# Five of eight batches' queries turned through DRAM instead of one, returning in two lots, with GpSimd taking two of the four low parts

## What is computed

```python
x = x + xattn(v=ctx, k=ctx, q=layernorm(x), mask, W_merge, b_merge)
#   scores = q @ k^T / sqrt(512); masked scores = -1e9; att = softmax(scores)
#   atted = att @ v; result = einsum('bdl,ol->bdo', atted^T, W_merge) + b_merge
x = x + ffn(layernorm(x), clip_x, clip_down, w_gate, w_up, w_down)
#   xq = fake_quant(x); h = fake_quant(silu(xq @ Wg^T) * (xq @ Wu^T)); h @ Wd^T
#   weights are fake-quantised row by row, activations by one scale over all 8 batches
```

## Time and profile before

| | us |
|---|---|
| median of 3 runs | 531.74 |
| lowest, highest | 531.61, 533.95 |
| the profiled execution's own time | 531.5 |
| its span, first to last instruction | 529.7 |
| PE busy | 522.4 (99%) |
| DVE busy | 440.1 (83%) |
| ACT busy | 302.2 (57%) |
| POOL busy | 151.0 (29%) |
| TensorE clock granted, mean | 1.000 of 2.4 GHz |

### The profile page before, as it was taken

The page is one execution under the profiler, slowest core; times in us unless marked ns, Lnnn a source line. Parts: engine busy times, 40 slices in busy tenths (PEclk is TensorE's granted clock), DMA queues, the critical chain, the costliest instruction groups (busy, mean ns, idle before and its releaser), DMA issues. The chain is left out here.

```text
span 529.7 us, 7450 instructions
## 1 busy us (share of the span) xinstructions
PE 522.4 (99%) x2481; PEld 347.0 (66%) x2481; DVE 440.1 (83%) x825; ACT 302.2 (57%) x455; POOL 151.0 (29%) x101
## 2 busy tenths in 40 slices
PE   7999999999999999999999999999999999999997
PEld 6888788888888888888888444444444445444444
DVE  5798999969799698898678678778788787699985
ACT  4795766657647565576433754653654533977620
POOL 2369556555457453663231000000000000000000
PEclk9999999999999999999999999999999999999999
DMA  8929569885884957756467639677301101869785
GB/s 271 262 101 162 189 170 165 255 177 175 197 149 175 223 173 179 178 199 188 103 89 189 239 94 283 244 203 228 112 8 40 40 0 30 341 251 395 270 285 197
DMA packets 80768, 95.71 MB, mean 181 GB/s; under 512 B 36448, under 2 KB 57312, under 8 KB 78176
## 3 DMA queue, kind: packets, MB, share of 16 engines
q1 hardware_dynamic: 80592, 95.24, 64.6%
q10 hardware_dynamic: 144, 0.07, 0.0%
HBM read 60.82 MB, written 26.48 MB: 165 GB/s over the span
## 5 line engine op out<-in xcount | busy, mean ns | idle before, releaser
L1528 PE MATMUL gu<-hid,gu_T 128*128 128x512 f16 x496 | 111.3, 379 | 0.1
L1528 PEld LDWEIGHTS gu<-hid,gu_T 128*128 128x128 f16 x496 | 48.4, 98 | 58.9 <-DVE hid L1394 0.6
L1295 ACT ACTIVATE hid<-gu,gu_mul 128x512 f32<-128x512 f32 x63 | 43.2, 685 | 53.8 <-PE gu L1528 46.8
L1394 DVE SCALAR_TENSOR_TENSOR hid<-gu,gu_mul,hid 128x512 f32 (+1 forms) x63 | 47.0, 748 | 28.4 <-PE gu L1528 16.2
L1410 DVE TENSOR_REDUCE hmax<-hid 128x1 f32 (+2 forms) x48 | 52.7, 1110 | 1.3 <-DVE hid L1394 1.3
L1333 ACT ACTIVATE h<-hid,inv 128x512 int8<-128x512 f32 (+3 forms) x35 | 44.3, 1343 | 11.7 <-DVE gu_T L1447 11.7
L493 ACT ACTIVATE probs<-probs,nmax 128x512 f32<-128x512 f32 x32 | 23.0, 720 | 45.7 <-DVE nmax L692 45.7
L968 PE MATMUL mm<-cT_hi,qT_hi 128*128 128x512 f32 x124 | 48.8, 393 | 0.0
L970 PE MATMUL mm<-cT_hi,qT_lo 128*128 128x512 f32 x124 | 48.3, 390 | 0.0
L969 PE MATMUL mm<-cT_lo,qT_hi 128*128 128x512 f32 x124 | 48.3, 389 | 0.0
L968 PE MATMUL mm<-g_hi,c_hi 128*128 128x512 f32 x124 | 48.2, 389 | 0.0
(11 more groups left out here) (196 smaller groups left out, 1047.0 us busy)
## 6 DMA issues: line engine op xcount, KB each, us to landing
h_dram<-hid SPq DMA_DIRECT2D x3, 2816.0 KB, 9.3
hid<-h_dram SPq DMA_DIRECT2D x3, 2816.0 KB, 11.5
cb<-in_ctx_dram SPq DMA_DIRECT2D x28, 256.0 KB, 8.0
cx<-in_ctx_dram SPq DMA_DIRECT2D x7, 1024.0 KB, 10.7
x<-in_x_dram SPq DMA_DIRECT2D x5, 1024.0 KB, 6.1
x_dram<-x SPq DMA_DIRECT2D x20, 256.0 KB, 2.8
xq<-x_dram SPq DMA_DIRECT2D x5, 1024.0 KB, 10.4
x<-x_dram SPq DMA_DIRECT2D x5, 1024.0 KB, 5.0
```

What stands on the lines that cost most here:

```text
L1295: nc.scalar.activation(silu[SILU_AT[i]], gu[2 * (i % 3)][:], ACT.Silu, scale=gu_mul[:, 0, i:i + 1]).then_inc(silu_done, 1)
L1394: nc.vector.scalar_tensor_tensor(hid[:, b % SLOTS, i * L:(i + 1) * L], gu[2 * (i % 3) + 1][:], gu_mul[:, 1, i:i + 1], silu[SILU_AT[i]], AL ...
L1528: last = nc.tensor.matmul(gu[2 * (i % 3) + g][:], gu_T[:, g, h, i * P:(i + 1) * P], xT[p][:, h, :], start=h == 0, stop=h == T - 1)
```

## The change

Batches 3 to 7 now take the way over DRAM (batch 2 and those before it don't). The queries of a batch come back in two lots of two tiles, four DMAs of 128 KB each, in place of four times four DMAs of 64 KB. SP's order becomes: all four tiles out, x1 tiles 0 and 1 stored, lot 0 back, x1 tiles 2 and 3 stored, lot 1 back, and then x of n+2 as before. Low parts 0 and 1 stay on DVE; 2 and 3 go to POOL, behind `make_c_lo(n)` and ahead of `make_rstd2(n-1)`. `norm1` of the next batch waits for both pairs of low parts.

```diff
-    BLOCK_Q = range(B - 1, B)
+    BLOCK_Q = range(B - 5, B)
...
+                def block_halves(n):
+                    return T // 2 * (n - BLOCK_Q[0])
...
-                    def queries_back(n, t):
-                        pieces = q_dram[n - BLOCK_Q[0], t * P:(t + 1) * P, :].rearrange("(k j) (a f) -> a j k f", j=BLK, f=P)
-                        sp.wait_ge(q_out[t], 16 * (n - BLOCK_Q[0] + 1))
+                    def queries_back(n, h):
+                        rows = slice(h * T // 2 * P, (h + 1) * T // 2 * P)
+                        pieces = q_dram[n - BLOCK_Q[0], rows, :].rearrange("(t k j) (a f) -> a j t k f", j=BLK, k=P // BLK, f=P)
+                        for t in HALF_ROWS[h]:
+                            sp.wait_ge(q_out[t], 16 * (n - BLOCK_Q[0] + 1))
                         for a in range(P // BLK):
-                            sp.dma_start(qn[a * BLK:(a + 1) * BLK, t, :].rearrange("j (k f) -> j k f", f=P),
-                                         pieces[a]).then_inc(q_back[t], 16)
+                            sp.dma_start(qn[a * BLK:(a + 1) * BLK, h * T // 2:(h + 1) * T // 2, :].rearrange(
+                                "j t (k f) -> j t k f", f=P), pieces[a]).then_inc(q_back[h], 16)
...
                     def queries_by_blocks(n):
-                        for t in range(T - 1):
+                        for t in range(T):
                             queries_out(n, t)
+                        for t in HALF_ROWS[0]:
+                            store_x1(n - 2, t)
                         queries_back(n, 0)
-                        queries_out(n, T - 1)
-                        for t in range(1, T):
-                            queries_back(n, t)
+                        for t in HALF_ROWS[1]:
+                            store_x1(n - 2, t)
+                        queries_back(n, 1)
...
                             if n + 1 in BLOCK_Q:
                                 queries_by_blocks(n + 1)
-                            for t in range(T):
-                                store_x1(n - 1, t)
+                            else:
+                                for t in range(T):
+                                    store_x1(n - 1, t)
...
+                    def block_query_lo(n, t):
+                        gp.wait_ge(q_hid, block_queries(n) + t + 1)
+                        nc.gpsimd.tensor_tensor(columns(qT_lo, t), blocks(qn[:, t, :]), columns(qT_hi, t).bitcast(F32),
+                                                ALU.subtract).then_inc(q_split_far, 1)
...
                         make_c_lo(n)
+                        if n + 1 in BLOCK_Q:
+                            for t in HALF_ROWS[1]:
+                                block_query_lo(n + 1, t)
                         if n:
                             make_rstd2(n - 1)
...
                     def block_query_turn(n, t):
-                        dve.wait_ge(q_back[t], 64 * (n - BLOCK_Q[0] + 1))
+                        if t % (T // 2) == 0:
+                            dve.wait_ge(q_back[2 * t // T], 64 * (n - BLOCK_Q[0] + 1))
                         nc.vector.transpose(qn[:, t, :], qn[:, t, :]).then_inc(q_turned, 1)
...
-                                if n + 1 in BLOCK_Q and k >= T // 2:
-                                    for t in HALF_ROWS[k - T // 2]:
+                                if n + 1 in BLOCK_Q and k == T // 2:
+                                    for t in HALF_ROWS[0]:
                                         block_query_lo(n + 1, t)
                                 mixed_lo(n, k)
...
                         if n in BLOCK_Q:
-                            pe.wait_ge(q_split, block_queries(n) + k + 1)
+                            if k < T // 2:
+                                pe.wait_ge(q_split, block_halves(n) + k + 1)
+                            else:
+                                pe.wait_ge(q_split_far, block_halves(n) + k - T // 2 + 1)
```

More of the change, by code:

```diff
@@ L155, in attention @@
                 t_done, t_hi, t_lo = sem("t_done"), sem("t_hi"), sem("t_lo")
-                q_out, q_back = [sem(f"q_out{t}") for t in range(T)], [sem(f"q_back{t}") for t in range(T)]
-                q_turned, q_hid, q_split = sem("q_turned"), sem("q_hid"), sem("q_split")
+                q_out, q_back = [sem(f"q_out{t}") for t in range(T)], [sem(f"q_back{h}") for h in range(2)]
+                q_turned, q_hid = sem("q_turned"), sem("q_hid")
+                q_split, q_split_far = sem("q_split"), sem("q_split_far")
                 wm_done, wm_hid, wm_ready = sem("wm_done"), sem("wm_hid"), sem("wm_ready")
@@ L279, in queries_out, with next_x @@
                         sp.dma_start(q_dram[n - BLOCK_Q[0], t * P:(t + 1) * P, :], qn[:, t, :]).then_inc(q_out[t], 16)
-                    def queries_back(n, t):
-                        pieces = q_dram[n - BLOCK_Q[0], t * P:(t + 1) * P, :].rearrange("(k j) (a f) -> a j k f", j=BLK, f=P)
-                        sp.wait_ge(q_out[t], 16 * (n - BLOCK_Q[0] + 1))
-                        for a in range(P // BLK):
-                            sp.dma_start(qn[a * BLK:(a + 1) * BLK, t, :].rearrange("j (k f) -> j k f", f=P),
-                                         pieces[a]).then_inc(q_back[t], 16)
+                    def queries_back(n, h):
[3 more added lines that the diff above has]
+                            sp.wait_ge(q_out[t], 16 * (n - BLOCK_Q[0] + 1))
+                        for a in range(P // BLK):
+                            sp.dma_start(qn[a * BLK:(a + 1) * BLK, h * T // 2:(h + 1) * T // 2, :].rearrange(
+                                "j t (k f) -> j t k f", f=P), pieces[a]).then_inc(q_back[h], 16)
+                    def next_x(n):
+                        if n:
+                            sp.wait_ge(min2, T * n)
+                            sp.wait_ge(x_free[(n - 1) % 3], 64 * ((n - 1) // 3 + 1))
+                        else:
+                            sp.wait_ge(wm_done, T)
+                        load_x(n + 2)
                     def queries_by_blocks(n):
-                        for t in range(T - 1):
+                        for t in range(T):
                             queries_out(n, t)
+                        for t in HALF_ROWS[0]:
+                            store_x1(n - 2, t)
                         queries_back(n, 0)
-                        queries_out(n, T - 1)
-                        for t in range(1, T):
-                            queries_back(n, t)
+                        for t in HALF_ROWS[1]:
+                            store_x1(n - 2, t)
+                        queries_back(n, 1)
                     def load_x(n):
@@ L361, in _ @@
                                 queries_by_blocks(n + 1)
-                            for t in range(T):
-                                store_x1(n - 1, t)
+                            else:
+                                for t in range(T):
+                                    store_x1(n - 1, t)
                         if n < B - 2:
[L365 to L370, removed]
+                            next_x(n)
                             sp.wait_ge(cT_ready, T * (n + 1))
@@ L517, in norm1 @@
                             if n - 1 in BLOCK_Q:
-                                act.wait_ge(q_split, block_queries(n))
+                                act.wait_ge(q_split, block_halves(n))
+                                act.wait_ge(q_split_far, block_halves(n))
                             else:
```

## The result

| | before | after |
|---|---|---|
| median, us | 531.84 | 538.76 |
| lowest, highest | 531.61, 533.95 | 537.52, 541.09 |
| profiled execution | 531.5 | 537.52 |
| its span | 529.7 | 535.7 |
| ratio after / before, 95% interval | | 1.0138 [1.0114, 1.0161] |

The changed kernel is 1.4% slower. The forecast was 531.8, with a range up to 536, so the time lies outside it.

The account below looks back on a forecast made before the run. PE was taken to bound the kernel; its 7.1 us gain would return as 7.0 of waits for the DVE-ACT loop, and -0.1 + 0.1 left 531.5 for the profiled execution, 531.8 as median, range 528.5 to 536.

Parts of the forecast that it names:

- What bounds the kernel: PE sets the pace; low part 0 was ready only 0.6 us before `scores(7)`, the cover of the DVE-ACT loop.
- Part 1: PE in steps 2 to 5: losing the transposes gives back 1.78 us each, 7.1 us in all.
- Part 2: The DVE-ACT loop paces once its cover is gone; PE's gain returns as waits, 7.0 of 7.1 us.
- M: Start of the first `mask_and_max` on DVE in a step, the point from which the loop's period is counted.
- the gain stands: Rival: moving low parts 2 and 3 off DVE shortens the loop, 526.9, or 524.4 if hidden altogether; chance 0.14.
- the held cast: DVE's cast is held by POOL, ending 1.04 us after the first `add_bias` ends, 1.25 in an odd step.
- The cast slips in first: Rival: POOL's low parts over 1.5 us each let the cast precede `add_bias`; 0.65 less per loop, 529.1; chance 0.10.
- the bounds for `variances2`: DVE's `variances2` beside POOL's low part 3: either nothing, or 0.25 us late each step, 1.0 in all; 0.1 taken.
- A: Start of `g_lo` 0 on DVE in a step, the point that splits the loop into two stretches.
- Part 3: Transfers on SP: lot 0 issued by M + 19.3, landing in 3.3 us where 4.7 was allowed; no delay.
- the lots are late: Rival: landing beyond 4.7 us delays the turn and all behind it in five steps, 538 to 548; chance 0.16.
- The end: Behind `scores(7)`: M is some 0.7 us late against PE, x1 and z loads off PE's path; costed at nothing.

Follow-up runs that it names:

- Experiment 7: The changed kernel without the queries' DRAM transfers and without DVE's turns, high parts starting when `norm1` is done; 523.54 us, ratio 0.9857 to the kernel before.
- Experiments 6: The changed kernel with the way over DRAM for batches 2, 4 and 6 only, PE transposing 3, 5 and 7; 531.35 us, ratio 1.0001 to the kernel before.
- 10: The changed kernel with only batches 4 and 6 over DRAM, `add_bias` behind DVE's cast; 529.78 us, ratio 0.9969 to the kernel before.
- experiment 1: The changed kernel without the queries' DRAM transfers, DVE turning the blocks as ACT wrote them; 532.96 us, ratio 1.0047 to the kernel before.
- experiment 3: The changed kernel with all four low parts on DVE; 536.87 us, ratio 1.0138 to the kernel before.
- experiment 8: The changed kernel without the queries' transfers, GpSimd's `add_bias` waiting for DVE's cast; 530.2 us, ratio 0.9985 to the kernel before.
- experiment 11: The changed kernel with unread filler matmuls on PE before `scores(4)` to `scores(7)`; 537.64 us, ratio 1.0124 to the kernel before.
- 12: The whole changed kernel, transfers included, with `add_bias` waiting for DVE's cast; 538.67 us, ratio 1.0123 to the kernel before.
- 2: The kernel before, with queries of batches 3 to 6 also copied through DRAM unread and batch 7 as in the changed kernel; 544.36 us, ratio 1.028.

## Why the prediction was wrong, point by point

**What bounds the kernel: right.** PE paced before, and the cover of the loop was 0.6 us. Experiment 7 shows it from the other side.

**Part 1, 4 x 1.78: right.** Experiments 6 and 10 have steps of 32.64, and experiment 7 turns the whole of it into time.

**Part 2, the loop: right.** Forecast were M to M of 34.45 and 34.65; the kernel after has 34.47 and 34.88 where no lot is late, and waits of 2.04, 1.76 and 1.75 before `scores(4)` to `scores(6)` against 1.2, 2.0 and 1.8 (in the first of them the cover was already gone by the late lot of step 2; experiment 1, without it, has 1.40, 1.79 and 1.75). That low parts 2 and 3 are off the path is shown by experiment 3, so *the gain stands* fell; the held cast by experiment 8. *The cast slips in first* didn't happen: the cast took 2.07 with `add_bias` ahead of it. Of the bounds for `variances2` the upper one was true: DVE's tiny instruction was held until GpSimd's second low part ended, at 215.77, and took 0.52 in place of 0.17. POOL after, step 5 (L446 its two low parts, L423 `make_rstd2`, which waits for `variances2`):

```profile
213.20 2.54 POOL L446 TENSOR_TENSOR qT_lo<-qn,qT_hi 128x512 fp32r<-128x512 f32 x2 [6.21 <-ACT qT_hi L503]
215.85 1.01 POOL L423 TENSOR_TENSOR ln<-ve,minus_half 128x4 f32<-128x4 f32 x1
```

Of these 0.35 some 0.15 reach the loop: `add_bias` started at 216.83, A + 9.47, forecast 249.3 - 239.98 = 9.32, and A to the next M is 11.97 and 11.75 where 11.8 and 11.6 were forecast.

**Part 3, the lots: wrong, and the step that failed is "so lot 0 is issued by M + 19.3".** That sum runs to the end of the lot's four DMAs (16.2, two stores and four DMAs of about 0.5), and it has no wait for the outs in it. They were costed by the 2.0 of the earlier trace rows, from a step in which the weights had been issued 6 us ahead. Where the outs did land in 2.0, the sum was right: in step 3 the lot's issue ended at 132.57 + 2.10 = 134.67, M + 19.6 (M is 115.10), and no turn waited. In steps 2 and 6 the weights were issued right ahead of the outs, the outs took 7.0 and 5.5, and SP stood 2.9 and 2.1 us for them. The lot's issue ended at M + 22.6 in step 2 (98.52 + 1.80 - 77.69) and at M + 21.4 in step 6 (238.90 + 1.80 - 219.33). From there to the turn it took 3.9 and 4.3 us, more than the 3.3 of "nearest to the first two: I take 3.3 us, no delay", but less than the 4.7 that the text could allow: from M + 19.3 such a landing would have been in time. So the wait for the outs, put at nothing, made the lots late; the landing, mis-sized by 0.6 to 1.0 (a piece took 3.7 to 4.7, not 2.1), made them a little later. That even steps load their weights behind the transpose of `w_down` could have been read from the code, and from the kernel before, whose step 2 has the weights at 90.88, M + 12.1; I looked at what is queued behind the lots, not at what is ahead of the outs.

**The rival *the lots are late* is what happened, in two steps of five, but not by its condition.** It asked for a landing of over 4.7, had 6 us in all five steps, at 1.3 each, and gave 538. The landing of lot 0, counted in the same way, stayed under 4.7, and the issue was late. Two steps at 1.7, one more wait for lot 1 in each, and the clock came to nearly the same time: the rival's number is right by chance, what it says of the turn (it waits, and everything behind it stands) by the trace.

**The clock: missed.** A wait of PE was costed at its length. The one of 3.52 us cost 1.66 more in the matmuls behind it (experiment 11).

**The end: mis-sized.** I cost it at nothing. It was 1.3 us in the kernel after, and 1.6 in experiment 1. ACT and PE after, at the last batch's z, and ACT there before (columns as in the earlier trace rows):

```profile
292.09 2.93 ACT L637 ACTIVATE xq<-xq,z_add,ln 128x512 f32<-128x512 f32 x4 [8.47 <-DMA xq<-x_dram]
...
292.95 2.77 PE L1118 MATMUL zt<-ident,xq 128*128 128x128 f32 x16 [0.30 <-ACT xq L637]
...
285.56 2.93 ACT L616 ACTIVATE xq<-xq,z_add,ln 128x512 f32<-128x512 f32 x4 [6.95 <-DMA xq<-x_dram]
```

ACT waited 8.47 us for the load of x1, and PE for ACT; before, it was 6.95 and PE didn't wait. "Off PE's path" was wrong for this load. SP issued it 21.5 us behind M(7) in both kernels and in experiment 1 (277.75, 272.96, 274.03). In the kernel after that was no later against PE than before, but ACT could start 14.3 us behind the issue, not 12.6. In experiment 1, M(7) was 0.7 late against PE and the load took 13.7. So the lateness that I had costed at nothing has a price, and why the load takes longer no run tested.

**The sum again,** with what was measured: low part 0 of step 2 came 34.0 after `scores(2)`, forecast 32.0 (the turn's 1.77 and 0.2); from there to low part 0 of step 6 140.7, forecast 138.2 (1.66 for the turn of step 6, 0.3 for lot 1 in step 2, 0.5 for GpSimd's later `add_bias`). That is 4.5, then 1.66 for the clock and 1.3 for the end.

**What stays open.** Why `w_down`'s transposes land later in the kernel after than before, so that the weights of step 6 are issued at M + 12.2 and not at M + 6.3; the traffic of the lots is the obvious suspect, and in experiment 1, which has none of it, they were issued at M + 8.8 (226.90 - 218.09), so it can be a part of it at most. How late the lots are from one execution to the next, since each kernel's trace is of one. Why the load at the end lands later.

## What to carry to other kernels

Work taken off the bounding engine is worth no more than the cover of the next loop: measure the period of the other engines' loop from one point to the same point, not their busy time, and give the relief to every second step, so that the loop can catch up in between (experiment 10). Ahead of a transfer that somebody waits for, look at what the same queue issues in the microseconds before it, in each kind of step: landing times belong to the place they were read at. Where a transfer may only be issued when another has landed, that landing is a term of its issue time.

## What the runs showed of the hardware

- A 256 KB store from SBUF landed in 2.0 us, and in 4.7 (step 4) to 7.0 when 1 MB of loads had been issued some 1 us ahead of it.
- TensorE's granted clock was 0.50 for some 3 us at or just behind the end of waits of 3.17 (experiment 3), 3.41 and 5.37 (12), 3.52 (the kernel after: 12.5 us for a product of 10.88) and 7.69 us (2), and stayed at 1.00 after waits of 2.04 and, in experiment 3, of 2.59.
- DVE's tiny `variances2` (128x4) took 0.52 us while GpSimd ran a subtraction and ended with it, 0.17 otherwise; the int8 cast took 2.0 with `add_bias` running and 1.23 without (2048 columns), 2.08 and 1.43 (2432).
- A step of PE with a wait in it shows 32.8 to 32.9 us of busy time, one without 32.64.
